# The second order of the edges made by moving groups of four records, in a graph network kernel

## The reference

```
GCN (two convolutions):  agg = segment_sum((h@W)[src] * dinv[src]*dinv[dst], dst)
GAT (4 heads):           e = leaky_relu(a_src[src] + a_dst[dst]); m = segment_max(e, dst)
                         out = segment_sum(h[src] * softmax_by_dst(e), dst)
Attention (8 heads):     a = (q[src].k[dst]/4 + mlp(edge_length)) * cut(edge_length)
                         out = segment_sum(softmax_by_src(a) * v[dst], src)
Messages:                agg = segment_sum([x[src], x[dst]] @ W_msg + b, dst); upd = [x, agg] @ W_upd
```

## Time and profile before

| | |
|---|---|
| timed, median of 3 | 11,506.52 us |
| span of the profiled execution | 14,964.0 us (the profile gives no other time of it) |
| busy in the span: PE, DVE, ACT, POOL | 7,438.9, 7,981.8, 2,323.4, 6,615.4 us |
| mean granted TensorE clock | 0.637 of full speed |
| DMA | 1,673 MB, mean 112 GB/s |
| indirect DMAs by line | L897 (scatters) 3136, L983 31, L1316 1664, L2145 1664 |

### The profile page before, as it was taken

How to read it: one execution, slowest core, us unless ns; L and a number is a source line. 1 busy time by engine, 2 the same in 40 slices (tenths; PEclk the granted TensorE clock), 3 DMA queues, 4 the chain that set the end, 5 groups by cost and what they waited for, 6 DMA issues and landing times. The chain is left out here.

```text
span 14964.0 us, 180024 instructions
## 1 busy us (share of the span) xinstructions
PE 7438.9 (50%) x37569; PEld 5659.3 (38%) x37570; DVE 7981.8 (53%) x21837; ACT 2323.4 (16%) x6049; POOL 6615.4 (44%) x6504
## 2 busy tenths in 40 slices
PE   5444444411066664339539200026655666666669
PEld 4333333411056664214215100025554555555444
DVE  7555555520078889300200799966665666666631
ACT  0101001000012220000100100002213444444300
POOL 0555555567700000370470377765543555555400
PEclk9555555555555555559659555556767888887789
DMA  0000000010066666318218466656662222222347
GB/s 26 1 1 1 1 1 1 1 31 1 10 184 197 196 195 175 103 40 297 90 40 311 130 203 202 204 173 205 210 176 76 83 82 83 83 82 83 62 166 263
DMA packets 1114463, 1673.21 MB, mean 112 GB/s; under 512 B 287476, under 2 KB 828112, under 8 KB 1075632
## 3 DMA queue, kind: packets, MB, share of 16 engines
q1 hardware_dynamic: 543264, 1032.94, 20.8%
q0 software_dynamic: 234960, 339.86, 8.9%
q10 hardware_dynamic: 335808, 296.39, 6.8%
HBM read 1263.13 MB, written 405.27 MB: 111 GB/s over the span
## 5 line engine op out<-in xcount | busy, mean ns | idle before, releaser
L1316 POOL DMA_INDIRECT big<-tab_h,idx x1664 | 1838.7, 1105 | 1478.2 <-DMA tab_h<-asrc 624.5
L2145 POOL DMA_INDIRECT big<-tab_kv,idx x1664 | 1593.8, 958 | 1389.5 <-PE banks L2220 477.7
L897 POOL DMA_INDIRECT by_dst<-idx,loc x832 | 856.3, 1029 | 2842.9 <-POOLq L2439 2589.9
L897 POOL DMA_INDIRECT by_src<-big,h x1568 | 1508.6, 962 | 1192.6 <-DVE h L619 742.9
L1659 PE MATMUL banks<-big,h 128*128 128x448 f32 x2744 | 1245.0, 594 | 750.9 <-issue 731.1
L1418 DVE SCALAR_TENSOR_TENSOR acc<-big,room,acc 128x1280 f32<-128x1280 f32 (+1 forms) x960 | 1378.8, 1512 | 23.6 <-DMA big<-cells 23.6
L1690 DVE COPY acc<-banks 128x448 f32<-128x448 f32 x18 | 11.2, 624 | 2509.7 <-PE banks L1659 2508.2
L1190 DVE SCALAR_TENSOR_TENSOR acc<-acc,h,banks 128x128 f32<-128x128 f32 x3966 | 1082.8, 341 | 496.9 <-DMA cells<-acc 247.9
L1659 PEld LDWEIGHTS banks<-big,h 128*128 128x128 f32 x2744 | 561.6, 205 | 1433.5 <-issue 1412.0
L2220 PE MATMUL banks<-big,room 128*128 128x136 f32 x3328 | 705.7, 346 | 680.4 <-DVE acc L2317 636.1
L1541 PE MATMUL banks<-big 128*128 128x132 f32 x3328 | 705.4, 379 | 469.5 <-DVE acc L1566 299.3
(11 more groups left out here) (467 smaller groups left out, 13976.1 us busy)
## 6 DMA issues: line engine op xcount, KB each, us to landing
big<-cells SPq DMA_DIRECT2D x262, 1568.0 KB
cells<-acc SPq DMA_DIRECT2D x1985, 64.0 KB
cells<-acc ACTq DMA_DIRECT2D x1984, 64.0 KB
big<-cells ACTq DMA_DIRECT2D x196, 640.0 KB
head_rows<-big SPq DMA_DIRECT2D x416, 264.0 KB
big<-head_rows SPq DMA_DIRECT2D x208, 528.0 KB
acc<-w_rows SPq DMA_DIRECT2D x208, 512.0 KB
big<-loc_rows SPq DMA_DIRECT2D x208, 256.0 KB
```

What stands on the lines that cost most here:

```text
L897: pool.indirect_dma_start(self.target, bass.IndirectOffsetOnAxis(self.slots[:, t:t + 1], axis=0), self.rec[:, t, :], None).then_inc(self.s ...
L1316: pool.indirect_dma_start(k.stage[:, m % BODY, :], None, k.tab_h_dram, bass.IndirectOffsetOnAxis(k.idx[:, m:m + 1], axis=0)).then_inc(k.ga ...
L2145: pool.indirect_dma_start(far[:, m % (G * RING), 0:2 * C], None, k.tab_kv_dram, bass.IndirectOffsetOnAxis(k.idx[:, m:m + 1], axis=0)).then ...
```

## The change

The 1568 scatters by destination go (736 beside the cells, 832 beside the two gathers), and with them the destination records and places. A record by source now also carries its place in the other order. Every cell is rounded up to a multiple of four records, so four neighbouring records of the list by source are always one cell's, and their place in the other order is one 64-byte row. At the head of the phase of cells POOL loads the list by source in nine chunks and writes each group of four with one descriptor: 432 indirect DMAs of 128 groups. Empty records are filled with a place behind the table. `NG` becomes 864, `T` 1728, `QJ` 32, and the loop of cells has 128 turns, 108 of them with units.

```diff
-NG = -(-((E + NB * (GE - 1)) // GE) // GB) * GB
+UNIT = 4
+NG = -(-((E + NB * NB * (UNIT - 1) + NB * (GE - 1)) // GE) // (2 * GB)) * (2 * GB)
...
-LATER = 832
-QJ = 31
+QJ = 32
...
+            pool.iota(spare, pattern=[[1, T]], base=P * T, channel_multiplier=T).then_inc(iotas, 1)
...
-            dve.memset(k.src_rec[:, :, 3], 0.0)
+            dve.tensor_copy(k.src_rec[:, :, 1], k.raw_s)
...
+            link(dve, dve.tensor_scalar(groups_i, k.cell_count[0:NB1, :], float(UNIT - 1), None, ALU.add))
+            link(dve, dve.tensor_scalar(groups_i, groups_i, UNIT.bit_length() - 1, None, ALU.arith_shift_right))
+            link(dve, dve.tensor_scalar(whole, groups_i, float(UNIT), None, ALU.mult))
```

The end of a turn of the ranks, where eight operations become three:

```diff
-            link(dve, dve.tensor_tensor(self.place[:, 1, :], self.rank, self.pick[:, 0, :], ALU.add))
-            link(dve, dve.tensor_tensor(self.place[:, 0, :], self.place[:, 1, :], self.pick[:, 1, :], ALU.add))
-            link(dve, dve.tensor_copy(self.place_i, self.place))
-            dve.tensor_scalar(self.low_i, self.place_i, P - 1, None, ALU.bitwise_and)
-            link(dve, dve.tensor_scalar(self.shift_i, self.place_i, 7, None, ALU.arith_shift_right))
-            dve.tensor_copy(self.low_f, self.low_i)
-            link(dve, dve.tensor_copy(self.shift_f, self.shift_i))
-            dve.scalar_tensor_tensor(self.slots[:, :, bass.ds(i * ROUND_COLUMNS, ROUND_COLUMNS)], self.low_f, float(TD),
-                                     self.shift_f, ALU.mult, ALU.add).then_inc(self.slotted, 1)
+            at = bass.ds(i * ROUND_COLUMNS, ROUND_COLUMNS)
+            link(dve, dve.tensor_tensor(self.place, self.rank, self.pick[:, 0, :], ALU.add))
+            dve.tensor_copy(k.pos[:, at], self.place)
+            dve.tensor_tensor(k.src_rec[:, at, 3], self.place, self.pick[:, 1, :], ALU.add).then_inc(self.slotted, 1)
```

The moves, a new class:

```diff
+    def fetch(self, pool, c):
+        if c >= 4:
+            last = (c - 3) * CHUNK // HALF
+            for r in range(self.SETS):
+                self.landed(pool, r, (last - r + self.SETS - 1) // self.SETS)
+        pool.dma_start(self.k.moved[c % 4], self.blocks[:, c * CHUNK:(c + 1) * CHUNK, :]).then_inc(self.fetched[c % 4], 16)
+
+    def gpsimd(self, pool):
+        k = self.k
+        for c in range(2):
+            self.fetch(pool, c)
+        for c in range(CHUNKS):
+            if c + 2 < CHUNKS:
+                self.fetch(pool, c + 2)
+            pool.wait_ge(self.fetched[c % 4], 16 * (c // 4 + 1))
+            pool.tensor_scalar(k.move_to[c % 4], k.moved[c % 4][:, :, 3], 1.0 / UNIT, None, ALU.mult)\
+                .then_inc(self.pointed, 1)
+            pool.wait_ge(self.pointed, c + 1)
+            for j in range(CHUNK):
...
+                pool.indirect_dma_start(
+                    k.by_dst_dram, bass.IndirectOffsetOnAxis(k.move_to[c % 4][:, j:j + 1], axis=0),
+                    k.moved[c % 4][:, j, :], None).then_inc(self.moved[r], 16)
```

In the phase of cells (now `cells_phase`) the list by source is loaded row by row, four tiles ahead, stored from one copy, and turned back by PE; two lists are stored for the attention layer before `taken`:

```diff
-            scatter.gpsimd(pool, 0, EC - LATER, extra=cell_rows)
+            cell_rows(pool)
+            moves.gpsimd(pool)
...
-            sp.dma_start(rec, k.by_src_dram.rearrange("(p t) f -> p t f", p=P)[:, 0:T, :]).then_inc(loaded, 16)
+            for m, at, n in tiles[0:4]:
+                load(m, at, n)
...
+            sp.wait_ge(staged, 2)
+            sp.dma_start(k.src_loc_dram, src_loc).then_inc(listed, 16)
+            sp.dma_start(k.src_idx_dram, src_idx).then_inc(listed, 16)
...
+                    last = pe.matmul(frm[:, u * P:(u + 1) * P], k.inc_from[:, j + u:j + u + 1].to_broadcast([P, P]),
+                                     k.ident[:, :], start=False, stop=True)
```

```diff
-        run(gather_phase, "gcn1", k.h, k.strips, k.total, (0, LATER // 2))
+        run(gather_phase, "gcn1", k.h, k.strips, k.total)
...
-        run(gather_phase, "gcn2", k.h, k.strips, k.total, (LATER // 2, LATER))
+        run(gather_phase, "gcn2", k.h, k.strips, k.total)
...
-        run(lists_phase, "dst")
+        run(dst_list_phase)
...
-        run(lists_phase, "src")
+        run(src_list_phase)
```

More of the change, by code:

```diff
@@ L326, in _ @@
         def _(act):
[L328 to L336, removed]
+            act.wait_ge(filled, 1)
+            for rows in (k.by_src_dram, k.by_dst_dram[0:P * MOVES, :]):
+                act.dma_start(rows.rearrange("(p r) f -> p (r f)", p=P), pattern).then_inc(zero_done, 16)
+            act.wait_ge(zero_done, 32)
         @block.gpsimd
@@ L891, in gpsimd @@
+    def gpsimd(self, pool, slotted):
+        k = self.k
+        for t in range(EC):
+            if t % ROUND_COLUMNS == 0:
                 pool.wait_ge(slotted, t // ROUND_COLUMNS + 1)
[L892 to L895 removed]
+            turn, r = divmod(t // HALF, self.SETS)
+            if t % HALF == 0 and turn:
                 pool.wait_ge(self.scattered[r], turn * HALF * 16)
@@ L1283, in _, with dst_list_phase, by_tile @@
                 dve.tensor_copy(w[:, :], k.psum[3][:, m * C:(m + 1) * C])
-def lists_phase(nc, k, which):
-    loaded = k.sem("lists_loaded")
-    full = {"dst": 2, "src": 4}[which]
-    source = {"dst": k.by_dst_dram, "src": k.by_src_dram}[which]
-    rec = k.acc[:, 0:T * full].rearrange("p (t f) -> p t f", f=full)
+def dst_list_phase(nc, k):
+    loaded, made, kept, turned, indexed, flipped = (k.sem("dst_list_" + n) for n in (
+        "loaded", "made", "kept", "turned", "indexed", "flipped"))
+    link = Link(k.sem("dst_list_step"))
+    full = T // P
+    rest = T - full * P
+    size = TILES * P
+    rec = k.big[:, 0:4 * size]
+    fields = rec.rearrange("t (x f) -> t x f", f=4)
+    at = 4 * size
+    low, pad, loc = (k.big[:, at + m * size:at + (m + 1) * size] for m in range(3))
+    low = low.bitcast(I32)
+    idx = k.acc[:, 0:size]
+    loc_bf = k.acc[:, size:size + size // 2].bitcast(BF16)
+    rows = k.by_dst_dram[0:P * MOVES, :].rearrange("(t q u) f -> t (q u f)", t=T, u=UNIT)
+    tiles = [(m, m * P, min(P, T - m * P)) for m in range(TILES)]
+    def by_tile(flat):
+        return flat.rearrange("t (m q) -> t m q", q=P)
     with nc.Block() as block:
@@ L1294, in _ @@
         def _(sp):
-            sp.dma_start(rec, source.rearrange("(p t) f -> p t f", p=P)[:, 0:T, :]).then_inc(loaded, 16)
+            sp.dma_start(rec[:, 0:full * 4 * P].rearrange("t (m x) -> t m x", m=full),
+                         rows[0:full * P, :].rearrange("(m t) x -> t m x", t=P)).then_inc(loaded, 16)
+            if rest:
+                sp.dma_start(rec[0:rest, full * 4 * P:TILES * 4 * P], rows[full * P:T, :]).then_inc(loaded, 16)
+            sp.wait_ge(made, 1)
+            sp.dma_start(k.loc_rows_dram[0:full * P, :].rearrange("(m t) q -> t m q", t=P),
+                         by_tile(loc_bf)[:, 0:full, :]).then_inc(kept, 16)
@@ new lines, in _ @@
+            if rest:
+                sp.dma_start(k.loc_rows_dram[full * P:T, :], loc_bf[0:rest, full * P:size]).then_inc(kept, 16)
+            sp.wait_ge(kept, 32 if rest else 16)
+        @block.tensor
+        def _(pe):
+            for done, flat, bank in ((made, loc, 0), (indexed, idx, 4)):
+                pe.wait_ge(done, 1)
+                for m, at, n in tiles:
+                    ins = pe.transpose(k.psum[bank + m // 4][:, m % 4 * P:m % 4 * P + n], flat[0:n, at:at + P],
+                                       k.ident[0:n, 0:n])
+                ins.then_inc(turned, 1)
@@ L1345, in maximum_phase @@
     steps = [(c, src) for c in range(len(spans)) for src in range(NB)]
-    turns = [(lo, min(4, T // P - lo)) for lo in range(0, T // P, 4)]
     with nc.Block() as block:
@@ L1611, in _, with gather_phase @@
             steps(dve, step)
-def gather_phase(nc, k, name, rows, strips, total, later=None):
+def gather_phase(nc, k, name, rows, strips, total):
     n = name + "_"
```

277 lines of the change are left out of this document (156 added, 121 removed).

## The result

The changed kernel takes 11,855.88 us (median of 4 runs, 11,833.43 to 11,877.84) against 11,516.31 for the kernel before, measured beside it: a ratio of 1.0299, 95% interval 1.0274 to 1.0324. The prediction said 11,675, slower, and its range ended at 11,790. The sign was right and the size half of what came.

A forecast was written before the change was run, and what follows sets the result against it. It took scatters to bound the ranks, DVE and stores the cells, POOL's gathers the maximum, group loops weighted and attention. Terms summed to +186 us, times 0.918 = +171, so 11,675 us, 1.5% slower; range 11,300 to 11,790.

The forecast's parts named there:

- The stall: Ranks, cells and both gathers: PE, DVE and ACT stand still beside POOL's scatters; 2,428 us in the trace, none assumed timed.
- Rival 1: Gathers and cells: part of the stall is real in timed runs, so the change is faster, 11,310 at the bound; chance 0.24.
- Scaling by 0.918: Whole kernel: the +186 us sum was multiplied by timed median over the span without the stall, giving +171.
- Longer lists: Loops over groups: 3.85% more groups at each phase's mean price, weighted +48.6, attention +107.5, and cells' turns +64 us.
- The four turns of the cells: Loop of cells: 124 turns become 128, four more with units at 15.9 us each, +64 us.
- Moves at nothing: Phase of cells: 432 indirect DMAs, some 580 us of POOL, hidden behind the loop of cells, price 0.
- Rival 4: Loop of cells: the moves' 64-byte writes disturb its stores, +60 us, 11,735 to 11,760; chance 0.06.
- Ranks at nothing: Ranks: 1568 scatters by source set the length, so DVE's saving of some 93 us is hidden, price 0.
- Rival 3: Ranks: DVE's chain sets the length instead of scatters, -93 x 0.918, giving 11,590, still slower; chance 0.10.
- Small terms: List by destination +25, list by source -7, fields -8, count and incidence +1, copies of later records -3 us.
- The queues beside the stall: Ranks: during 98 stalled turns 14 instruction packets moved in 2,500 us and the scatters' queue was busy 2%.
- Rival 2: Whole kernel: the costs cancel and the time does not change, 11,510 us; chance 0.10.

The follow-up runs named there:

- e1: The kernel before, unchanged, profiled a second time: span 11,509.7 us.
- e6: Changed kernel with lists at their old length and empty records pointing to different rows: 11,458.86 us, ratio 0.9948 to the kernel before.
- e5: Changed kernel, long lists kept, with empty records pointing to different rows: 11,784.2 us, ratio 1.0237 to the kernel before.
- e16: Changed kernel with old-length lists, empty records pointing to different rows and 64 idle instructions on DVE: 11,463.36 us, ratio 0.9933.
- e12: Changed kernel, long lists, with empty records pointing to different rows and 64 idle instructions on DVE before attention: 11,651.8 us, ratio 1.0104.
- e2: Changed kernel with lists at their old length (NG 832, QJ 31, chunks of 32): 11,482.42 us, ratio 0.9964 to the kernel before.
- e11: Changed kernel with 64 idle instructions on DVE ahead of attention: 11,762.21 us, ratio 1.0195 to the kernel before.
- e13: Kernel before with 64 idle instructions on DVE ahead of attention: ratio 0.9979 to the unedited kernel before.
- e7: Kernel before with list columns given padding rows 0 to 831, the same row for all 128 partitions: 11,484.46 us, ratio 0.9969.
- e3: Changed kernel without the 432 moves and their loads, list by destination left empty, GAT rows wrong: 13,962.05 us, ratio 1.2109 to the kernel before.
- e14: Changed kernel with 32 idle instructions on DVE ahead of attention: 11,740.42 us (one run).
- e15: Changed kernel with 128 idle instructions on DVE ahead of attention: 11,881.15 us (one run).
- e8: Changed kernel with 32 idle instructions on ACT ahead of attention: 11,872.85 us, ratio 1.0291 to the kernel before.
- e10: Changed kernel with 96 idle instructions on ACT ahead of attention: 11,892.6 us, ratio 1.0308 to the kernel before.

## Why the prediction was wrong

**The stall was taken as none in the timed run: right**, and more so than the text dared. By the rows alone it bounded the share left at 0.31; e1 shows zero. Rival 1 is dead, and with it the 0.24 for faster and the low end of the range. What failed is "The stall will be there again", and the span near 13,880 that followed. Of the phases without the stall the ranks were read well, 2,000 against 2,016.0 measured. The gathers, thought to be 557 by their scatters, took 536, so their gain of -32 was in fact -7.3. The scatters ran at 1.26, the faster end of what the text had allowed, and did not set the phase.

**Scaling by 0.918** treated all other phases as slowed alike. Attention was 2,796.3 in the earlier trace rows and 2,160.4 in e1, a factor of 0.77, weighted 1,264 and 1,047.0, 0.83, while the maximum hardly moved. So 3.85% of attention is 83 us and not the 99 of the forecast.

**Longer lists** is the step that failed, in two ways. It priced a group at the phase's mean, 143 us for weighted and attention together, and they grew by 302.
- *Length itself* was about right: e6 to e5 gives 44 for weighted (predicted 48.6 x 0.918 = 45), e16 to e12 gives 77 for attention (predicted 99).
- *What the added records are* was left out. They are empty and read one row each time, so they cost more than the mean: weighted loses 67.6 to this with the long lists (e5) and 7.7 with the short ones (e2 to e6), so the longer lists brought 60 of its +102.3. With 44 for length and the -1.9 between e1 and e2 that is the whole. The 60 rests on single traces and is good to some 20 us.
- *Where the loop's code lies* was left out. Moving DVE's code takes 103.3 us off attention in the changed kernel (e11), and spreading the rows 34.8 more (e12). At the short lists the two together are worth nothing (2,144.0 in e2, 2,144.5 in e16). So the +199.6 are 77.4 for length, 138.1 for the two costs, and -16.4 between e1 and e2, which is no more than two traces differ by. The kernel before pays some 25 for its own gap (e13), so the gap at the branch is not new with the change; new are the second stop and the price.

"Attention's extra groups are cheaper than its mean" was what the text feared; they were dearer.

**The four turns of the cells**: +64 x 0.918 = 59 forecast. e2 to the changed kernel, 2,075.3 to 2,124.3, gives 49. From e1 to e2 the phase falls by 24.9, forecast -10 for its head; but e7, whose cells are those of before, took 2,073.2 as well, so this fall isn't shown. Together +24.1 measured, +50 forecast.

**Moves at nothing: right.** e3 shows it. They ran from 2412.2 to 3020.2, 1.41 us each where 1.26 to 1.4 was forecast:

```profile
L933 POOL DMA_INDIRECT by_dst<-x,h x432: 957/971/2150, 2412.2 to 3020.2; - x144
```

They were done earlier than forecast, since the cells start at 2334 and not near 3080. Rival 4 is dead.

**Ranks at nothing: nearly right.** DVE's busy time fell by 75 us and the phase grew by 12, paced by 1568 scatters in both:

```profile
L885 POOL DMA_INDIRECT by_src<-big,h x1568: 957/962/2444, 330.4 to 2322.0; - x196
```

Rival 3 is dead. Why a scatter's median is 962 ns here and 958 in e1 was not tried; 4 ns x 1568 are 6 of the 12 us.

**Small terms.** List by destination +25 forecast, +20.1 measured; list by source -7, -6.5; fields -8, -9.8; all right.

**The queues beside the stall** say nothing of its cause. In the ranks of the stalled execution 14 instruction packets moved in the 2,500 us from 500, and the scatters' queue was busy 2.0%; in e1, whose ranks have no stall, they were 16 packets and 2.7% in the 1,800 us from 500. The stall kept whole in the timed run, 10,500, is refuted by e1. Instruction packets were looked at only where engines stood still beside scatters; in the attention phase of both kernels they were many, 283 and 273, and DVE stood still beside them.

**Rival 2**, costs that cancel, is dead with the interval. Measured less forecast (341.8 - 171), phase by phase: weighted 102.3 - 44.6 = 58, attention 199.6 - 98.7 = 101, gathers -7.3 + 29.4 = 22, ranks 12, other phases held to be untouched 6 (4.9 + 3 - 1.8), cells 24.1 - 49.6 = -26, the small terms -3: together 170. By cause, padding that reads one row is some 60 of it in weighted and 35 in attention, and DVE's gap 103; neither was a term of the sum. Against them stand 21 by which attention's length was priced too high and the 16 between e1 and e2.

## What to carry to other kernels

Trace a kernel twice before a stall is believed; a span 30% above the timed median is reason enough. When a change makes a list longer, ask what the added entries are and which addresses they read: padding that reads one row was worth 68 us of the weighted phase, and pointing it to different rows costs some 2 us here (the list by destination took 33.1 us in e5, 30.8 before). After any change of length compare the packets of the instruction queue and the gap at each loop's branch, since the place of the code was worth 103 us in a phase to which the longer lists themselves added 77. Compare a phase in several traces of unchanged code before a difference of 10 or 20 us is given a cause.

The idea of the change holds: with this graph's lists kept at 832 groups and the padding spread (e6) it beats both kernels as they stood, at 0.9948. Against the kernel before with its own padding changed (e7, 0.9969) the intervals overlap, so how much of that is the moves' is not shown. That form drops the bounds that make the lists hold any graph, which is what the change paid for with its longer lists.

## What the runs showed of the hardware that was not expected

- A gather of 128 rows took 3.08 us when all are the same row and 1.46 when they are rows of the graph (e3, maximum phase; 1,024 each, the phase's length divided by them). The moved bytes are the same, 299.42 MB; the DMA's rate fell from 200 to 95 GB/s while the busy share of its engines rose from 0.64 to 0.74.
- 32 idle instructions on VectorE took 110 us off the attention phase of 2,360, and 128 took nothing off (e14, e15). A DVE loop beside which instruction packets came, 283 in the phase where the moved code had 22, stood still at its branch for 3 to 4 us (198.2 us in 54 turns), while moving ACT's code made no difference (2,365.4 to 2,372.2, e8 to e10). With one such stop a turn and POOL setting the pace it cost nothing (2,144.0 us in e2 against 2,144.5 in e16); with a second, of some 1.7 us, it came with the 103 us.
- The longest stop at DVE's branch was 15.8 us with padding that reads one row and 3.8 with different rows (the changed kernel and e5).
- One execution in the study stalled the other engines beside its indirect scatters, and no other did: its ranks, cells and two gathers took 752, 898 and 935 us more than those of e1, the same kernel.
